# Two-layer cross attention on one core: the second layer's engine orders rewritten, with a new share-out of its copies

## The chip, the cores and the metric

The kernel runs on one core of one Trainium2 chip. The metric is device time in microseconds (us) of one execution; shorter is better. The engines of the core are named as the profile names them: PE is TensorE (matmuls and transposes), ACT is ScalarE, DVE is VectorE, POOL is GpSimd, SP is SyncE, which here only issues DMAs. Each engine runs its own instructions strictly in the order in which they are written, and waits on semaphores for the others. Two layers run one after the other with an MLP between them; the change touches only the last part, which takes the final third of the time.

## What is computed

There are 16 entries. Each has 128 rows of 512 numbers, `x`, and 128 context rows of 512. The first layer is a cross attention with MLP, which this change leaves alone. The second takes its result `x` and does, for `b, l, s = 4, 256, 256` in the reference, which for a mask of zeros and the kernel's own split of the data is 16 entries of 128 by 128:

```python
q = hidden_state @ Wq + bq              # 32 heads of 16
k = encoder_hidden_state @ Wk + bk      # 8 heads of 16, each shared by 4 query heads
v = encoder_hidden_state @ Wv + bv
scores = jnp.einsum('bkgld,bksd->bkgls', q, k) * scale
scores = scores + encoder_attention_mask[:, :, None, :, :]
attn = jax.nn.softmax(scores, axis=-1)
out = jnp.einsum('bkgls,bksd->bkgld', attn, v)
out = out.transpose(0, 3, 1, 2, 4).reshape(b, l, H)
out = out @ Wo + bo
x = out + hidden_state
mu = jnp.mean(x, axis=-1, keepdims=True)
var = jnp.var(x, axis=-1, keepdims=True)
return (x - mu) * jax.lax.rsqrt(var + EPS) * gamma + beta
```

## The kernel before

The second layer is `second_attention` (L1236). One entry is a chain of steps that goes from engine to engine. Numbers are kept in fp32, and a product of two of them is made of three passes over halves (`hi` and `lo`: a rounded copy and what the rounding left off), so nearly each matrix is written twice, `hi` by ACT and `lo` by DVE. The steps of an entry, by the functions' names:

- `turn`: PE transposes the entry's rows into bank `G[1]`; ACT writes `hThi`, DVE writes `hTlo`.
- `query`: PE, 12 matmuls of 512 columns into `G[0]`; DVE adds the bias into `Qn`. `turn_query`: PE transposes `Qn`, ACT writes `QThi`, DVE `QTlo`.
- `context`: PE, 12 matmuls of 256 columns into `G[1]` (keys and values together); DVE adds the biases (`Cn`, `V`). `turn_context`: one transpose, ACT writes `KThi`, DVE `KTlo`.
- `scores(r)`, r = 0 and 1: PE, 24 matmuls on four row strips that fill the four banks `S`. Each round feeds four steps `k`, so an entry has eight.
- `mask_max(k)` on DVE adds the mask and takes the maximum of four heads; `exp(k)` on ACT does four exponentials with their sums; `probs(k)` on PE turns the four 128x128 blocks of `pr` into bank `O` (even `k`) or `T` (odd `k`); `copy(k)` brings them into `pT`. Even copies are DVE's, odd ones ACT's.
- `invert(r)`: DVE takes the reciprocals of the sums `den`, each written 16 times over, 128x256 (L1555). `inverse(r)`: PE turns them into `G[r]`; `spread(r)`: ACT copies them into `inv` (L1455).
- `values(r)`: PE, 8 small matmuls into `G[r]`, the same bank; `attended(r)`: DVE multiplies by `inv` into `an` (L1568), and POOL makes `aThi` and `aTlo`.
- `output`: PE, two halves of 6 matmuls into `G[1]`; DVE adds the residual into `res`. `moments`, `root` (POOL, Newton steps on 128x1), `norm`, `affine` (POOL) finish the entry, and SP stores it.

The order of each engine is written out by hand in its `period(b)`. A period works on three or four entries at once: `before` is b-1, `after` b+1. The periods of b = -1, 0, 1 and 14, 15, 16 are written out; the twelve between run in a loop of two periods. The two `G` banks serve ten uses of an entry, and every use waits until the one before it in that bank has been read, by wait lines in the functions. The PE order puts `scores(after, 0)` behind both halves of `output(before)`, then `inverse(b, 0)`, `probs(b, 5)`, `values(b, 0)`, `probs(b, 6)`, `turn(b+2)`; `query` is the second step of the next period. ACT has `spread(b, 0)` behind `exp(b, 5)` and `turn_context`, and three exponentials' steps or copies behind it. DVE has `turn(b+2)`, `moments(before)` and `attended(b, 0)` near the end of its period, and the two reciprocals between masks.

Of the kernel before, what the change touches and what calls it, by code (L numbers as in the profile page):

```python
# [28 lines left out]
ALU = mybir.AluOpType  # L29
# [3 lines left out]
B, R, H = 16, 128, 512  # L33
# [1190 lines left out]

def all_periods(eng, period):

    for n in (-1, 0, 1):
        period(Entry(n))
    with eng.Fori(0, (B - 4) // 2) as it:
        period(Entry(2, it))  # L1230
        period(Entry(3, it))
    for n in (B - 2, B - 1, B):
        period(Entry(n))


def second_attention(nc, top, staging, ident, handed, banks, mask, q_b, k_b, v_b, o_b, norm_w, norm_b, out):  # L1236
# [14 lines left out]
    with st:  # L1251
# [19 lines left out]
        rec = [sb(f"rec{r}", [P, RC * EIGHT, DH1]) for r in range(ROUNDS)]  # L1271
# [15 lines left out]
        a_seen, moments_seen, scores_seen = map(sem, ("a_seen", "moments_seen", "scores_seen"))  # L1287
# [6 lines left out]
        SMALL = 3  # L1294

# [8 lines left out]
        with nc.Block() as block:  # L1304

            @block.sync
            def _(sp):
                def load_context(e):
                    for h in range(2):
# [3 lines left out]
                def load_mask(e):  # L1313
                    sp.dma_start(madd[e.s][:, :], mask[e.index(), 0]).then_inc(mask_loaded[e.s], 16)

                def load_rows(e):
                    sp.dma_start(y_rows[e.s][:, :], kept_y[e.index()]).then_inc(y_loaded[e.s], 16)
# [4 lines left out]

                def period(b):
                    if b.exists() and b.plus(2).exists():
                        sp.wait_ge(resid_ready, b.count(1, 1))
                        sp.wait_ge(turned, b.count(1, 1))
                        load_rows(b.plus(2))
                        sp.wait_ge(c_full, b.count(1, 1))
                        load_context(b.plus(2))
                    if b.plus(-2).exists():  # L1330
                        store(b.plus(-2))
                    if b.exists() and b.plus(2).exists():
                        sp.wait_ge(masked, b.count(STEPS, STEPS))
                        load_mask(b.plus(2))
# [16 lines left out]
                store(Entry(B - 1))  # L1351
# [4 lines left out]
            def _(pool):  # L1356
# [22 lines left out]

                def root(e):  # L1380
# [18 lines left out]
                def period(b):  # L1399
                    if b.plus(-2).exists():  # L1400
                        root(b.plus(-2))
                    if b.plus(-1).exists():
                        attended(b.plus(-1), 1)
                    if b.plus(-2).exists():
                        affine(b.plus(-2))
                    if b.plus(1).exists():
                        residual(b.plus(1))
                    if b.exists():
                        attended(b, 0)

                all_periods(pool, period)
                root(Entry(B - 1))
                affine(Entry(B - 1))

            @block.scalar
            def _(act):
                def turn(e):
                    act.wait_ge(turned, e.count(1, 1))
                    nc.scalar.activation(hT[0][:, :, :], G[1][:, :].rearrange("p (k r) -> p k r", k=KC), ACT.Copy)\
                        .then_inc(h_hi, 1)  # L1420

                def turn_query(e):
                    act.wait_ge(qt_full, e.count(1, 1))
                    nc.scalar.activation(QT[e.s][0][:, :, :], G[0][:, :].rearrange("p (k r) -> p k r", k=KC),
                                         ACT.Copy, scale=scale).then_inc(q_hi, 1)

                def turn_context(e):
                    act.wait_ge(ct_full, e.count(1, 1))
                    for a in range(2):
                        last = nc.scalar.activation(KT[e.s][0][:, a, :], G[0][:, 0:R], ACT.Copy,  # L1430
# [14 lines left out]
                def copy(e, k):  # L1445
                    r, j = k // SB, k % SB
                    act.wait_ge(p_full[1], e.count(SB, k // 2 + 1))
                    wait(act, o_full, e.count(ROUNDS, r - 1))
                    nc.scalar.activation(pT[r][:, j, :, :, :].rearrange("p c a k -> p (c a k)"), PT[1][:, :], ACT.Copy)\
                        .then_inc(copied[1], 1)  # L1450

                def spread(e, r):
                    act.wait_ge(r_full, e.count(ROUNDS, r + 1))
                    wait(act, a_scaled, e.count(ROUNDS, r - 1))
                    nc.scalar.activation(inv[r][:, :], G[r][:, 0:RC * R], ACT.Copy).then_inc(r_spread, 1)  # L1455

                def period(b):
                    before, after = b.plus(-1), b.plus(1)
                    if b.exists():
                        exp(b, 0)  # L1460
                    if before.exists():
                        copy(before, 7)
                    if b.exists():
                        exp(b, 1)
                    if before.exists():
                        spread(before, 1)
                    if b.exists():
                        exp(b, 2)
                        copy(b, 1)
                        exp(b, 3)  # L1470
                    if after.exists():
                        turn_query(after)
                    if b.exists():
                        exp(b, 4)
                        copy(b, 3)
                        exp(b, 5)
                    if after.exists():
                        turn_context(after)
# [3 lines left out]
                    if b.exists():  # L1482
                        spread(b, 0)
                        exp(b, 6)
                        copy(b, 5)
                    if b.plus(2).exists():
                        turn(b.plus(2))
# [545 lines left out]
```

## Time and profile before

| | us |
|---|---|
| median of three runs | 1276.95 |
| lowest and highest | 1273.9, 1278.49 |
| the profiled execution's own time | 1279.8 |
| its span in the profile | 1278.0 |
| end of the MLP, last rows added up by DVE | about 861 |
| scores of entry 1 (first matmul) | 898.22 |
| scores of entry 15 (first matmul) | 1233.17 |

The span is what the profile covers; the execution's own time is 1.8 us longer, and both are of one execution. In a timeline row the first number is the start from the span's start, the second the length; a matmul's length includes its way through the array, so back-to-back matmuls overlap, and their pace is read from start to start. `[1.33 <-DVE KT0lo L1534]` says that the engine stood idle for 1.33 us before the row and that DVE's write of `KT0lo` released it. PEclk is the clock that TensorE was granted, as a share of its upper level of 2.4 GHz; the lower level is 1.2 GHz, a share of 0.5.

### The profile page before, as it was taken

The numbers are of one execution on the slowest core, as the hardware profiler recorded it, in microseconds if no ns is written. First come the engines' busy times: TensorE is split into PE (matmuls) and PEld (weight loads), VectorE is DVE, ScalarE is ACT, GpSimd is POOL, SyncE is SP. The second block draws the span as 40 slices with busy tenths as digits, with TensorE's granted clock in tenths as the row PEclk, the third lists the DMA queues.
The fourth block names the chain that finished last, engine by engine and source line by source line (L and its number), as shares of the span: only waits on it lengthen the run. The fifth ranks groups of instructions, "written<-read, shape, count | busy, mean of one in ns | idle before, by whom it ended". The sixth has DMA issues, their size and how long they took to land. (4 is left out here: it accounts for less than half of the span.)

```text
span 1278.0 us, 27329 instructions
## 1 busy us (share of the span) xinstructions
PE 1121.2 (88%) x8976; PEld 935.1 (73%) x8976; DVE 735.7 (58%) x2667; ACT 658.9 (52%) x2220; POOL 310.3 (24%) x475
## 2 busy tenths in 40 slices
PE   4899999999999975999999999996778778778774
PEld 3788888888888854898989989985556556556553
DVE  4577777777776755422212212215678778788784
ACT  4455555555555544533333333325677677677672
POOL 1223333332332331000000000000133333333334
PEclk8999999999999987999999999997889989989987
DMA  6212111112111005211001101404111111111100
GB/s 242 86 55 69 45 43 43 43 47 81 44 43 43 26 17 174 90 50 50 30 20 49 50 0 49 116 17 116 32 59 36 53 52 35 56 49 35 45 10 25
DMA packets 65349, 71.10 MB, mean 56 GB/s; under 512 B 7056, under 2 KB 41104, under 8 KB 65296
## 3 DMA queue, kind: packets, MB, share of 16 engines
q1 hardware_dynamic: 65296, 70.42, 17.5%
q8 instruction: 30, 0.49, 0.2%
q14 instruction: 23, 0.19, 0.1%
HBM read 49.43 MB, written 20.97 MB: 55 GB/s over the span
## 5 line engine op out<-in xcount | busy, mean ns | idle before, releaser
L689 POOL TENSOR_TENSOR pr<-pr,rec 128x512 f32<-128x512 f32 x128 | 130.6, 1042 | 297.2 <-DVE rec L947 297.2
L1441 ACT ACTIVATE pr<-pr,nmax 128x128 f32<-128x128 f32 x512 | 198.1, 392 | 0.8
L1921 ACT ACTIVATE g_m<-J,b_part_m 128x256 f32<-128x256 f32 x128 | 60.6, 474 | 217.9 <-PE J L162 217.9
L791 ACT ACTIVATE pr<-pr,nmax 128x256 f32<-128x256 f32 x256 | 126.6, 501 | 4.1 <-DVE nmax L936 4.0
L1548 DVE CUSTOM_DVE_ANT_0 pr<-S,madd 128x128 f32<-128x128 f32 x512 | 115.7, 284 | 14.3 <-PE S L1700 10.3
L1898 POOL TENSOR_TENSOR resid_m<-resid_m,b_all_m 128x512 f32<-128x512 f32 x16 | 23.1, 1464 | 329.7 <-DMA resid_m<-in_x 329.7
L1441 ACT ACTIVATION_READ_ACCUMULATOR pr<-pr,nmax 128x1 f32 x512 | 98.4, 192 | 0.0
L936 DVE CUSTOM_DVE_ANT_0 pr<-S,madd 128x256 f32<-128x256 f32 x256 | 92.6, 418 | 8.2 <-PE S L1127 8.1
L162 PE MATMUL J<-wqhi,hThi 128*128 128x512 f32 x128 | 65.1, 508 | 22.6 <-DVE wqlo L150 11.3
L162 PE MATMUL J<-nT0hi_m,uphi_m 128*128 128x256 f32 x256 | 73.2, 286 | 9.8 <-DVE uplo_m L150 8.9
L162 PE MATMUL J<-hThi,wkhi 128*128 128x256 f32 x256 | 75.4, 294 | 5.9 <-DVE wvlo L150 5.9
L162 PE MATMUL J<-nT0hi_m,uplo_m 128*128 128x256 f32 x256 | 72.7, 284 | 0.0
L162 PE MATMUL J<-nT0lo_m,uphi_m 128*128 128x256 f32 x256 | 72.6, 283 | 0.0
L1710 PE MATMUL T<-ident,pr 128*128 128x128 f32 x256 | 42.0, 289 | 34.5 <-ACT pr L1441 34.5
L162 PE MATMUL J<-hThi,wklo 128*128 128x256 f32 x256 | 72.0, 281 | 0.0
L162 PE MATMUL J<-hTlo,wkhi 128*128 128x256 f32 x256 | 72.0, 281 | 0.0
L162 PE MATMUL J<-nT1hi_m,uphi_m 128*128 128x256 f32 x256 | 71.8, 280 | 0.0
L162 PE MATMUL J<-nT1hi_m,uplo_m 128*128 128x256 f32 x256 | 71.6, 280 | 0.0
L162 PE MATMUL J<-nT1lo_m,uphi_m 128*128 128x256 f32 x256 | 71.5, 279 | 0.0
L1145 PE MATMUL S<-ident,pr 128*128 128x128 f32 x512 | 62.9, 277 | 0.0
L162 PE MATMUL J<-wqlo,hThi 128*128 128x512 f32 x128 | 61.8, 483 | 0.0
L1455 ACT ACTIVATE inv<-J 128x256 f32<-128x256 f32 x32 | 12.3, 384 | 94.2 <-PE J L1720 94.2
(232 smaller groups left out, 3323.1 us busy)
## 6 DMA issues: line engine op xcount, KB each, us to landing
staged<-in_L_xattn_mlp_w SPq DMA_DIRECT2D x16, 512.0 KB, 5.1
rows<-in_ctx SPq DMA_DIRECT2D x16, 256.0 KB, 2.8
rows<-in_x SPq DMA_DIRECT2D x16, 256.0 KB, 3.0
kept_c<-hThi SPq DMA_DIRECT2D x16, 256.0 KB, 2.6
kept_c<-hTlo SPq DMA_DIRECT2D x16, 256.0 KB, 2.8
kept_n<-n_out SPq DMA_DIRECT2D x16, 256.0 KB, 2.4
n_in<-kept_n SPq DMA_DIRECT2D x16, 256.0 KB, 3.7
resid_m<-in_x SPq DMA_DIRECT2D x16, 256.0 KB, 2.9
```

The costliest lines, as they stand in the source:

```text
L162: mm = nc.tensor.matmul(out, stationary(a, k), moving(b, k), start=first and k == 0 and (a, b) == PASSES[0], stop=last and k == chunks - 1 ...
L689: pool.tensor_tensor(part, part, by.unsqueeze(2).broadcast_to([P, per_bank, keys]), ALU.mult).then_inc(normed, 1)
L791: last = nc.scalar.activation(part, part, ACT.Exp, bias=nmax[slot][:, at], scale=-1.0, accum_out=den[slot][:, at])
L936: last = nc.vector.tensor_tensor_reduce(pr[slot][:, j, cols], S[j][:, cols], madd[s][:, :], -1.0, FAR, ALU.add, ALU.min, nmax[slot][:, j * ...
L1145: mm = nc.tensor.transpose(S[j][:, to * P:(to + 1) * P], pr[slot][:, j, q * P:(q + 1) * P], ident[:, :])
L1441: last = nc.scalar.activation(pr[k][:, i, :], pr[k][:, i, :], ACT.Exp, bias=nmax[k][:, i:i + 1], scale=-1.0, accum_out=den[r][:, at:at + 1])
L1455: nc.scalar.activation(inv[r][:, :], G[r][:, 0:RC * R], ACT.Copy).then_inc(r_spread, 1)
L1548: last = nc.vector.tensor_tensor_reduce(pr[k][:, i, :], S[j][:, i * R:(i + 1) * R], madd[e.s][:, :], -1.0, FAR, ALU.add, ALU.min, nmax[k][ ...
L1710: mm = nc.tensor.transpose(PT[t][:, i * R:(i + 1) * R], pr[k][:, i, :], ident[:, :])
L1898: pool.tensor_tensor(resid[t][:, :], resid[t][:, :], b2_all[:, :], ALU.add)\
L1921: nc.scalar.activation(g[slot][:, :], J[j][:, 0:PR], ACT.Gelu_apprx_tanh, bias=b1_part[:, f, :]).then_inc(J_taken[j], 1)
```

## The change

All of it is in the second layer.

1. **Orders.** The `period` functions of all five engines are rewritten with a helper `at(b, ahead, operation, ...)` that runs an operation for entry b+ahead if there is one. `query` and `turn` are now done two entries ahead, `query(b+2)` at the very end of PE's period; `spread(b, 0)` moves behind `exp(b, 6)`; `moments` moves from b-1 to b-2 and so to the next period; `attended(b-1, 0)` opens DVE's period. The periods run from b = -2 to 17, and ten of them are in the loop.
2. **Banks.** Which of the two `G` banks a use gets is now a table (`HOME`), and the wait before a use is worked out from the order of uses (`ORDER`, `EMPTIED`) by `free`. `inverse(0)` and `values(0)`, which shared a bank, now have one each, and `output` and `values(1)` do too; `values` has lost its own wait for `spread`.
3. **Copies.** `copy(3)` moves from ACT to DVE: three of eight are ACT's (1, 5, 7), five DVE's (0, 2, 3, 4, 6).
4. **Reciprocals.** DVE takes them on 128x16; POOL then writes each 16 times over into a new tile `wide` (`widen`), which PE turns.
5. **SP.** The loads of entry b+2 carry their waits with them and stand ahead of the store of b-2.
6. **Start and end.** The turn of entry 0 stood ahead of the weights on ACT, DVE and PE. It is now in the period of b = -2, behind the weights on ACT, and on DVE behind the waits for all the constants too.

```diff
+        HOME = dict(turn=1, query=1, turn_query=1, context=0, turn_context=0, inverse0=1, inverse1=0, values0=0,
+                    values1=0, output=1)
+        ORDER = (("inverse1", -1), ("turn_query", 1), ("values1", -1), ("turn", 2), ("context", 1), ("output", -1),
+                 ("turn_context", 1), ("inverse0", 0), ("values0", 0), ("query", 2))
...
+                def widen(e, r):
+                    pool.wait_ge(rec_ready, e.count(ROUNDS, r + 1))
+                    wait(pool, r_full, e.count(ROUNDS, r - 1))
+                    pool.nop().then_inc(rec_seen, 1)
+                    pool.tensor_copy(wide[r][:, :, :], rec[r][:, :].unsqueeze(2).broadcast_to([P, RC * EIGHT, DH1]))\
+                        .then_inc(rec_wide, 1)
...
                 def invert(e, r):
                     dve.wait_ge(exped, e.count(STEPS, SB * r + SB))
-                    nc.vector.reciprocal(rec[r][:, :, :], den[r][:, :].unsqueeze(2).broadcast_to([P, RC * EIGHT, DH1]))\
-                        .then_inc(rec_ready, 1)
+                    wait(dve, rec_wide, e.count(ROUNDS, r - 1))
+                    nc.vector.reciprocal(rec[r][:, :], den[r][:, :]).then_inc(rec_ready, 1)
...
             @block.vector
...
                 def period(b):
+                    at(b, 0, mask_max, 1)
+                    at(b, -1, attended, 0)
+                    at(b, 0, mask_max, 2)
+                    at(b, -1, copy, 6)
+                    at(b, -1, invert, 1)
+                    at(b, 0, mask_max, 3)
+                    at(b, 1, query)
+                    at(b, -2, moments)
+                    at(b, 0, copy, 0)
+                    at(b, 1, turn_query)
+                    at(b, 0, mask_max, 4)
+                    at(b, -1, attended, 1)
+                    at(b, 0, mask_max, 5)
+                    at(b, 2, turn)
+                    at(b, 0, mask_max, 6)
+                    at(b, 1, context)
+                    at(b, -2, norm)
+                    at(b, 0, invert, 0)
+                    at(b, 0, mask_max, 7)
+                    at(b, 0, copy, 2)
+                    at(b, 1, turn_context)
+                    at(b, 0, copy, 3)
+                    at(b, -1, output)
+                    at(b, 0, copy, 4)
+                    at(b, 1, mask_max, 0)
...
             @block.tensor
...
                 def period(b):
+                    at(b, -1, probs, 7)
+                    at(b, -1, inverse, 1)
+                    at(b, 0, probs, 0)
+                    at(b, 1, turn_query)
+                    at(b, 0, scores, 1)
+                    at(b, 0, probs, 1)
+                    at(b, -1, values, 1)
+                    at(b, 2, turn)
+                    at(b, 0, probs, 2)
+                    at(b, 1, context)
+                    at(b, -1, output, 0)
+                    at(b, 1, turn_context)
+                    at(b, 0, probs, 3)
+                    at(b, -1, output, 1)
+                    at(b, 0, probs, 4)
+                    at(b, 1, scores, 0)
+                    at(b, 0, probs, 5)
+                    at(b, 0, inverse, 0)
+                    at(b, 0, values, 0)
+                    at(b, 0, probs, 6)
+                    at(b, 2, query)
...
             @block.scalar
...
                 def period(b):
+                    at(b, 0, exp, 1)
+                    at(b, -1, copy, 7)
+                    at(b, -1, spread, 1)
+                    at(b, 1, turn_query)
+                    at(b, 0, exp, 2)
+                    at(b, 0, copy, 1)
+                    at(b, 2, turn)
+                    at(b, 0, exp, 3)
+                    at(b, 0, exp, 4)
+                    at(b, 1, turn_context)
+                    at(b, 0, exp, 5)
+                    at(b, 0, exp, 6)
+                    at(b, 0, spread, 0)
+                    at(b, 0, exp, 7)
+                    at(b, 0, copy, 5)
+                    at(b, 1, exp, 0)
...
             @block.gpsimd
...
                 def period(b):
+                    at(b, -1, attended, 0)
+                    at(b, -1, widen, 1)
+                    at(b, -2, root)
+                    at(b, -1, attended, 1)
+                    at(b, -2, affine)
+                    at(b, 0, widen, 0)
+                    at(b, 1, residual)
```

What this does to the instructions is seen at three places of the loop. `pr5_1` is the block of step 5, `inv0_1` the spread inverses of round 0, `J0` and `J1` are the banks `G[0]` and `G[1]`, and REGISTER_ALU rows compute what a wait compares with.

ACT around the spread of round 0, before:

```order
L1430 ACTIVATE KT1hi_1<-J0,parity_1 128x128 x2
L1453 REGISTER_ALU
L1455 ACTIVATE inv0_1<-J0 128x256
L1436 REGISTER_ALU
L1441 ACTIVATE pr6_1,den1_1<-pr6_1,nmax6_1 128x128 x4
L1447 REGISTER_ALU
L1449 ACTIVATE pT1_1<-T 128x512
L1418 REGISTER_ALU
L1419 ACTIVATE hThi_1<-J1 128x512
```

ACT in the same place after the change:

```order
L1455 ACTIVATE KT1hi_1<-J0,parity_1 128x128 x2
L1461 REGISTER_ALU
L1466 ACTIVATE pr5_1,den1_1<-pr5_1,nmax5_1 128x128 x4
L1461 REGISTER_ALU
L1466 ACTIVATE pr6_1,den1_1<-pr6_1,nmax6_1 128x128 x4
L1478 REGISTER_ALU
L1480 ACTIVATE inv0_1<-J1 128x256
L1461 REGISTER_ALU
L1466 ACTIVATE pr7_1,den1_1<-pr7_1,nmax7_1 128x128 x4
```

The exponentials of steps 5 and 6 now stand ahead of `inv0`, and the turn of the next rows (`hThi`) is no longer among what follows it.

PE behind the first scores of the next entry, before:

```order
L1720 MATMUL J0<-ident,rec0_1 128x128 x2
L1707 REGISTER_ALU
L1710 MATMUL T<-ident,pr5_1 128x128 x4
L1730 MATMUL J0<-pT0_1,V0_1 32x256 x8
L1707 REGISTER_ALU
L1222 REGISTER_ALU
L1710 MATMUL O<-ident,pr6_1 128x128 x4
L1658 REGISTER_ALU
L1222 REGISTER_ALU
L1661 MATMUL J1<-ident,y_rows0 128x128 x4
L1710 MATMUL T<-ident,pr7_1 128x128 x4
```

PE in the same place after:

```order
L1717 MATMUL T<-ident,pr5_1 128x128 x4
L1659 REGISTER_ALU
L1722 REGISTER_ALU
L1724 MATMUL J1<-ident,wide0_1 128x128 x2
L1734 MATMUL J0<-pT0_1,V0_1 32x256 x8
L1714 REGISTER_ALU
L1222 REGISTER_ALU
L1717 MATMUL O<-ident,pr6_1 128x128 x4
L162 MATMUL J1<-wqhi_1,hThi_1 128x512
```

The inverses now follow the block of step 5 and go into the other bank than the values; the query product of b+2 follows the block of step 6, where the turn of the rows and the block of step 7 stood.

DVE at the reciprocal of round 1, before:

```order
L1548 ISA nmax2_1 128x1
L1560 REGISTER_ALU
L1561 COPY pT1_1<-O 128x512
L1554 ISA
L1555 RECIPROCAL rec1_1<-den1_1 128x256
```

DVE in the same place after:

```order
L1559 ISA nmax2_1 128x1
L1571 REGISTER_ALU
L1222 REGISTER_ALU
L1573 COPY pT1_1<-O 128x512
L1565 ISA
L1567 RECIPROCAL rec1_1<-den1_1 128x16
L1559 ISA pr3_1,nmax3_1<-S3,madd0_1 128x128
```

The place is the same, the reciprocal is 16 elements wide in place of 256.

## Rows read from the trace of the kernel before

**Rows 1.** The page of the kernel before, its first line.

```profile
span 1278.0 us, 27329 instructions
```

**Rows 2.** Windows: start:end us, length, busy us (instructions) by engine, PEclk, DMA share, GB/s.

```profile
core 0: us, PE busy (x) PEld busy (x) DVE busy (x) ACT busy (x) POOL busy (x), PEclk, DMA share, GB/s
560.00:850.00 290.00, 290.00 (x1859) 261.35 (x1858) 60.32 (x121) 97.62 (x212) 16.36 (x12) 1.00 0.13 40
1043.20:1138.60 95.40, 74.98 (x645) 56.47 (x643) 75.02 (x352) 66.75 (x296) 33.49 (x77) 0.93 0.14 47
1045.00:1050.20 5.20, 1.76 (x13) 1.33 (x13) 2.58 (x11) 4.43 (x21) 0.00 (x0) 1.00 0.48 151
1050.20:1054.20 4.00, 4.00 (x11) 3.14 (x12) 4.00 (x21) 2.22 (x10) 3.13 (x13) 0.59 0.00 0
1054.20:1066.00 11.80, 10.16 (x93) 7.83 (x92) 10.74 (x52) 8.49 (x38) 4.00 (x6) 1.00 0.06 22
```

**Rows 3.** Timeline, PE, first scores of entries 1, 8, 9, 15: start us, us, engine.

```profile
898.22 0.59 PE L1700 MATMUL S<-KT1hi,QT1hi 32*128 32x256 f32 x4 [3.40 <-DVE KT1lo L1534]
...
1066.06 0.39 PE L1700 MATMUL S<-KT0hi,QT0hi 32*128 32x256 f32 x4 [1.33 <-DVE KT0lo L1534]
1089.86 0.39 PE L1700 MATMUL S<-KT1hi,QT1hi 32*128 32x256 f32 x4 [1.32 <-DVE KT1lo L1534]
...
1233.17 0.39 PE L1700 MATMUL S<-KT1hi,QT1hi 32*128 32x256 f32 x4 [1.25 <-DVE KT1lo L1534]
```

**Rows 4.** Timeline of one period, ACT and DVE rows behind the scores.

```profile
1067.45 0.38 ACT L1455 ACTIVATE inv<-J 128x256 f32<-128x256 f32 x1 [3.49 <-PE J L1720]
1070.62 0.60 ACT L1419 ACTIVATE hThi<-J 128x512 fp32r<-128x512 f32 x1 [0.77 <-PE J L1661]
...
1071.25 0.69 DVE L1505 TENSOR_TENSOR hTlo<-J,hThi 128x512 fp32r<-128x512 f32 x1 [3.04 <-ACT hThi L1419]
```

**Rows 5.** The tile `rec` and its readers: count, ns min/median/max.

```profile
L947 DVE RECIPROCAL rec<-den x64: 166/169/179, 48.5 to 467.9; 128x4 f32<-128x4 f32 x64
L1555 DVE RECIPROCAL rec<-den x32: 1741/1746/1750, 894.5 to 1255.9; 128x256 f32<-128x256 f32 x32
```

**Rows 6.** Lines by form, 1043.2 to 1138.6 us, DVE, then ACT.

```profile
L1561 DVE COPY pT<-O 128x512 f32<-128x512 f32 x16 | 10.8, 673 | 1.6 <-PE O L1710 1.6
...
L1441 ACT ACTIVATE pr<-pr,nmax 128x128 f32<-128x128 f32 x128 | 49.5, 393 | 0.3
L1449 ACT ACTIVATE pT<-T 128x512 f32<-128x512 f32 x16 | 9.3, 581 | 0.0
```

**Rows 7.** Timeline, PE, one period: query product and first half of output.

```profile
1050.18 0.47 PE L162 MATMUL J<-wqhi,hThi 128*128 128x512 f32 x1 [0.72 <-DVE an L1568]
...
1054.61 0.60 PE L1710 MATMUL O<-ident,pr 128*128 128x128 f32 x4
...
1061.17 0.47 PE L1743 MATMUL J<-wohi,aT0hi 128*128 128x512 f32 x1 [0.38 <-issue]
...
1062.63 0.27 PE L1690 MATMUL J<-ident,Cn 128*128 128x128 f32 x1
```

**Rows 8.** Lines by form, same stretch, POOL.

```profile
L1376 POOL CAST aT0hi<-an 128x256 fp32r<-128x256 f32 x4 | 1.6, 397 | 20.5 <-DVE an L1568 20.5
L1378 POOL TENSOR_TENSOR aT0lo<-an,aT0hi 128x256 fp32r<-128x256 f32 x4 | 3.0, 738 | 0.3
```

**Rows 9.** Timeline, start of the layer: PE, then DVE.

```profile
866.42 0.79 PE L162 MATMUL J<-wqhi,hThi 128*128 128x512 f32 x1 [4.03 <-DVE wqlo L150]
...
872.43 0.69 DVE L1512 TENSOR_TENSOR Qn<-J,bq_all 128x512 f32<-128x512 f32 x1 [4.93 <-DMA nb_all<-in_L_xattn_beta]
879.30 2.36 DVE L150 TENSOR_TENSOR wolo<-staged,wohi 128x1024 fp32r<-128x1024 f32 x2 [0.33 <-ACT wohi L145]
```

**Rows 10.** Timeline, end: last exponential on ACT, PE, then DVE.

```profile
1255.03 0.40 ACT L1441 ACTIVATE pr<-pr,nmax 128x128 f32<-128x128 f32 x1
...
1258.94 1.93 PE L1730 MATMUL J<-pT,V 128*32 128x256 f32 x16 [0.47 <-ACT inv L1455]
...
1266.56 0.69 DVE L1575 TENSOR_TENSOR res<-J,resid 128x512 f32<-128x512 f32 x1 [4.74 <-PE J L1743]
```

More of the change, by code:

```diff
@@ L1222, in wait, with at @@
         eng.wait_ge(sem, value)
+def at(b, ahead, operation, *which):
+    e = b.plus(ahead)
+    if e.exists():
+        operation(e, *which)
 def all_periods(eng, period):
-    for n in (-1, 0, 1):
+    for n in range(-2, 4):
         period(Entry(n))
[L1229 to L1232, printed above, removed]
+    with eng.Fori(0, (B - 6) // 2) as it:
+        period(Entry(4, it))
+        period(Entry(5, it))
+    for n in range(B - 2, B + 2):
         period(Entry(n))
@@ L1308, in load_context @@
                 def load_context(e):
+                    wait(sp, c_full, e.count(1, -1))
                     for h in range(2):
@@ L1321, in store, with first_two @@
                     sp.dma_start(out[e.index()], fin[e.s][:, :]).then_inc(stored[e.s], 16)
+                def first_two(e):
+                    return e.it is None and e.n < 2
                 def period(b):
[L1324 to L1334, printed above, removed]
+                    if not first_two(b.plus(2)):
+                        at(b, 2, load_context)
+                    if not first_two(b.plus(2)):
+                        at(b, 2, load_rows)
+                    if not first_two(b.plus(2)):
+                        at(b, 2, load_mask)
+                    at(b, -2, store)
                 for s in range(2):
@@ L1454, in spread @@
                     wait(act, a_scaled, e.count(ROUNDS, r - 1))
-                    nc.scalar.activation(inv[r][:, :], G[r][:, 0:RC * R], ACT.Copy).then_inc(r_spread, 1)
+                    nc.scalar.activation(inv[r][:, :], bank(f"inverse{r}")[:, 0:RC * R], ACT.Copy).then_inc(r_spread, 1)
                 def period(b):
[L1458 to L1478, printed above, removed]
+                    at(b, 0, exp, 1)
[14 more added lines that the diff above has]
+                    at(b, 1, exp, 0)
                     if b.it is None and b.n == -1:
@@ L1481, in period @@
                             staging.take_hi(nc, act, u, targets[u])
[L1482 to L1487, printed above, removed]
-                    if b.exists():
-                        exp(b, 7)
-                turn(Entry(0))
                 for u in QUERY + (CONTEXT,):
@@ L1652, in _, with free @@
                 all_periods(dve, period)
-                norm(Entry(B - 1))
             @block.tensor
             def _(pe):
+                def free(use, e):
+                    at_ = [name for name, _ in ORDER].index(use)
+                    b = e.plus(-ORDER[at_][1])
+                    for back in range(1, 3 * len(ORDER)):
+                        periods, n = divmod(at_ - back, len(ORDER))
+                        name, ahead = ORDER[n]
+                        user = b.plus(periods + ahead)
+                        if HOME[name] == HOME[use] and user.exists():
+                            sem_, per, more = EMPTIED[name]
+                            pe.wait_ge(sem_, user.count(per, more))
+                            return
                 def turn(e):
                     pe.wait_ge(y_loaded[e.s], e.uses(16))
-                    wait(pe, res_ready, e.count(1, -2))
+                    free("turn", e)
                     for k in range(KC):
-                        mm = nc.tensor.transpose(G[1][:, k * R:(k + 1) * R], y_rows[e.s][:, k * P:(k + 1) * P],
+                        mm = nc.tensor.transpose(bank("turn")[:, k * R:(k + 1) * R], y_rows[e.s][:, k * P:(k + 1) * P],
                                                  ident[:, :])
@@ L1724, in values @@
                 def values(e, r):
[L1725 removed]
+                    free(f"values{r}", e)
                     for t in range(2):
@@ L1775, in period @@
-                    if b.exists():
-                        probs(b, 4)
-                    if before.exists():
-                        output(before, 1)
-                    if after.exists():
-                        scores(after, 0)
-                    if b.exists():
-                        inverse(b, 0)
-                        probs(b, 5)
-                        values(b, 0)
-                        probs(b, 6)
-                    if b.plus(2).exists():
-                        turn(b.plus(2))
```

164 lines of the change are left out of this document (45 added, 119 removed).

## The prediction

> **What bounds the kernel now.** The span [rows 1] is read first, and of it only the last third can change. There the starts of the first scores give the beat: 898.22 us for entry 1, 1233.17 for entry 15 [rows 3], 14 periods of 23.9 us. Next comes the busy time in a stretch of four such periods, 95.40 us [rows 2]: PE 74.98, DVE 75.02, ACT 66.75, POOL 33.49, which is 18.7, 18.8, 16.7 and 8.4 us for one period of 23.85. No engine is full, so the period is a ring of waits. The timeline shows the ring. PE waits 1.33 us for `KTlo` at 1066.06. Behind those scores stand the inverses, and ACT has idled 3.49 us for them when it spreads them at 1067.45. ACT then does one step of exponentials and a copy, waits 0.77 us for the turned rows, writes `hThi` at 1070.62, and DVE, idle for 3.04 us, takes it at 1071.25 [rows 4]. From there DVE works nearly without a gap up to the next `KTlo` and the scores at 1089.86 [rows 3]. DVE's reciprocals lie in that last part.
>
> There is a second price. At the end of the idle part PE has been busy for 1.76 us of 5.20; its clock then stands at a share of 0.59 for 4 us, most of it the lower level, and the query product falls there [rows 2]. That product of 12 matmuls takes 4.43 us (1050.18 to 1054.61). Six matmuls of the same width take 1.46 us in the output (1061.17 to 1062.63), so twelve would take about 2.9 at the upper level [rows 7]. The wait thus costs 1.5 us more on PE in each period.
>
> **The change, part by part.** I first ask how short a period can be by each engine's own work, then whether the waits allow it.
>
> DVE. Two reciprocals of 1.746 us shrink to 128x16. The first layer's 128x4 form takes 0.169 us; the 252 elements between the two forms cost 1.577 us, so 12 more than four give 0.24 us [rows 5]. That takes off 3.0 us. One more copy adds 0.67 us as shown, some 0.60 from start to start [rows 6]. 18.8 - 3.0 + 0.6 = 16.4 us.
>
> ACT. One copy less, 0.58 us shown [rows 6], 0.5 in the queue: 16.7 - 0.5 = 16.2 us.
>
> PE. No matmul is added or dropped. If it no longer idles long, the query product is back at 2.9: 18.7 - 1.5 = 17.2 us. That counts the tails of matmuls before each idle piece; adding up starts in the dense part of a period gives some 16.5. So PE's floor is 16.5 to 17.2.
>
> POOL. Two widenings of 128x256 are new, in a form that the trace of before does not have. The nearest rows are a cast of 128x256 at 0.40 us and a subtraction with two inputs at 0.74 [rows 8]; I take 0.4, with 0.4 and 0.8 as ends, since the copy too has one input. POOL ends near 9.2 to 10 us, far below the others, and its cover matters only for who waits: `widen(1)` lies between DVE's reciprocal and PE's `inverse(1)`, and `widen(0)` behind `affine`.
>
> Do the waits allow some 17 us? I lay the two new orders of DVE and PE side by side, with the step lengths above and 0.2 us for a hand-over, and ask by how much PE's period must start later than DVE's. What DVE hands to PE asks for the following offsets: the reciprocal with its widening 3.6 us, `Qn` 3.7, `QTlo` 3.8, `an` of round 1 before the context product 4.0, `hTlo` before the output 4.0, `KTlo` before the scores 3.9. What PE hands to DVE allows at most: `values(1)` before `an` 4.3, the turned rows by way of ACT 4.3, the context product 4.4, the scores before the next `mask_max(0)` 4.3, the output before `res` 4.5. So an offset of 4.0 to 4.3 meets all of them. ACT needs 3.5 to 3.85 against DVE and may have at most 3.6, so it will stand a little at the spread, and it has 0.8 us of room for that in a period of 17. The step that held the ring before, the spread of round 0, now has `exp(6)` ahead of it, so its wait of 3.49 us is covered by an exponential step of about 1.5 us (four at 0.39 from start to start [rows 6]) and by the earlier inverses; what comes late next is PE's own queue. The windows are only 0.3 us wide, so I add a little and take 17.0 us a period, with 16.4 and 17.9 as its ends.
>
> The moved loads on SP cost nothing: rows and context of b+2 are asked for about a period before they are used. The store of b-2 now stands behind them; nobody waits for it except POOL two entries on.
>
> The start. The turn of entry 0 now waits for the last constant. DVE took that at 872.43 for `Qn` [rows 9]; it will now take it for `hTlo`, 0.7 us, then the query product follows, 4.4 us at the lower level as in [rows 7], where it had begun at 866.42 [rows 9]. `Qn` comes near 878, 5.5 us later. The turn of entry 1 now precedes the scores of entry 0, and the split of the output weights, 2.36 us on DVE at 879.30 [rows 9], now follows `mask_max(0)` and so holds up `mask_max(1)`. Against this, the query of entry 1 is already done. I take the scores of entry 1 at 904.5, 6.3 us later; ends 3 and 9.
>
> The end. In before, the last exponential starts at 1255.03 [rows 10], 21.9 us behind the scores of entry 15. In the new order ACT has its eight exponential steps (12.3 us), four smaller things (1.5) and short waits: it ends some 18.5 us behind those scores, 3.8 less with the reading-out of the sum. Of what follows up to 1278.0, 22.6 us, `invert` and `widen` take 0.7 instead of 1.75, so the values at 1258.94 [rows 10] come 1.1 us earlier; `output`, which ends with `res` at 1266.56 [rows 10], the moments, the root and the store stay. Scores of entry 15 to the end: 18.5 + 21.5 = 40 us, where it was 44.8.
>
> **The sum.** 904.5 + 14 x 17.0 + 40 = 1182.5 us of span, 95.5 less than before. With 1.8 us outside the span this is 1184.3 against the profiled execution's own 1279.8. That execution was 2.85 us above the median, so I forecast 1182 us (0.926 of before). The period's ends alone move it by -8 and +13 us, start and end by -4 and +4: 1172 to 1196.
>
> **Rivals.** *The clock falls once in each period.* For it: after the query product PE now has the blocks of steps 7, 0, 1 and 2, two small products, turned inverses, `Qn` and rows in one run of about 5 us before the next wide product, and the same kind of work left the clock at 0.59 behind 1045 to 1050.2. Against it: there PE stood idle for most of the time, and the dense stretch 1054.20 to 1066.00, with 10.16 of 11.80 us busy and a good third of that in transposes, was granted 1.00 [rows 2]. If it falls, the query product's 1.5 us come back, on context and output instead: 18.6 us a period, 1205 us. The Trainium skill speaks for this rival, in TensorE: Matmul & The Clock Gate, Part 4: PE-mode transpose: transposes do not count as activity for the clock as other matmuls do. The stretch at 1.00 does not bear it out, and the stretch before the fall cannot tell it from idleness.
>
> *The waits still make a ring and only the reciprocals' gain stays.* For it: three engines within 5% of each other, and windows of 0.3 us. Both reciprocals lie in the old ring, 3.0 us of it, and 23.9 - 3.0 = 20.9 would be left. 904.5 + 14 x 20.9 + 40 gives 1237 us as the worst of this case; anything between 18.5 and 21 us a period belongs to it or to the clock. Against it: the spread, which held the ring, has been passed by an exponential step, and the queue positions leave the slack counted above.
>
> *Slower.* PE stays at the lower level for most of every period, since many short waits of 0.1 to 0.3 us lie between its steps. At that level matmuls take twice as long from start to start, 16.5 us of work becomes up to 30 and the time 904.5 + 14 x 30 + 40 = 1364 us. It passes the old 23.9 when a bit more than half of PE's work falls at the lower level. Against it: the MLP, with PE always busy, had 1.00 for 290 us, and in the old period a gap of several us cost the clock for only 4 us of 24 [rows 2].
>
> *No gain.* The orders wait for something that I have overlooked, such as a load of SP or POOL's `root` ahead of `attended(1)`, and the period stays near 23.9; with the longer start it would be about 1278.
>
> **How the numbers follow.** Forecast (1172 to 1196): 0.60. Clock: 0.17. Ring: 0.15. Slower: 0.04. No gain: 0.03, and 0.01 is left for below 1172. The range reaches from 1169 up to 1215, which takes in the clock rival and the nearer part of the ring, 0.85 or so. A measurement can tell about 0.3% (4 us) from no change; faster by more than that 0.94, within it 0.02, slower 0.04.
>
> **What would show it.** Scores of one entry 17.0 us behind those of the last, PE busy for over 93% of the period at a share of 1.00, ACT's wait before `inv` below 0.6 us where it was 3.49, and DVE's before `hTlo` below 0.3 us. A query or output product that takes over 4 us is the clock rival. A DVE that is under 85% busy together with a PE under 90% is the ring, and the wait that is longest names it. `widen` above 0.8 us, or first scores of entry 1 outside 901 to 908, would make single terms wrong. The forecast as a whole is wrong if the period is above 17.9 us or below 16.4.

## The result, and the profile after

| | before | after |
|---|---|---|
| median, us | 1277.65 | 1174.83 |
| lowest and highest | 1273.9, 1278.49 | 1172.35, 1180.94 |
| runs | 4 | 4 |
| scores of entry 1, profiled execution | 898.22 | 906.43 |
| scores of entry 15 | 1233.17 | 1136.74 |
| one period between them, mean of 14 | 23.93 | 16.45 |
| from scores of entry 15 to the end | 44.8 | 38.0 |

The ratio is 0.921, with an interval of 0.917 to 0.925. The forecast was 1182 us. The profiled execution took 1176.46 us. Its span stands beside [rows 1]:

```profile
span 1174.7 us, 27388 instructions
## 1 busy us (share of the span) xinstructions
PE 1085.1 (92%) x8976; PEld 918.0 (78%) x8976; DVE 691.9 (59%) x2683; ACT 648.2 (55%) x2204; POOL 321.9 (27%) x507
```

The windows, with the columns of [rows 2]: twelve periods, then a short stretch that is rich in transposes, then all that follows the scores of entry 15.

```profile
939.34:1136.80 197.46, 197.25 (x1933) 156.05 (x1932) 190.99 (x1069) 191.58 (x877) 110.35 (x254) 1.00 0.20 64
1043.80:1046.62 2.82, 2.82 (x41) 2.38 (x40) 2.29 (x12) 2.82 (x13) 0.04 (x2) 1.00 0.00 0
1136.74:1174.70 37.96, 21.58 (x189) 13.64 (x188) 20.58 (x102) 19.09 (x89) 21.95 (x56) 0.86 0.08 29
```

In twelve periods PE stands still for 0.21 us, at a granted clock of 1.00 throughout. A period of 16.46 us holds 16.44 of PE, 15.9 of DVE, 16.0 of ACT and 9.2 of POOL. The ring of waits (each engine held up by another, round to the first) is gone, and the second layer runs at the pace of PE's own work. PE's timeline in the middle of it, where before every score stood behind a wait [rows 3] and the query product began behind one [rows 7]:

```profile
1038.07 0.39 PE L1707 MATMUL S<-KT1hi,QT1hi 32*128 32x256 f32 x4
...
1039.47 0.38 PE L1724 MATMUL J<-ident,wide 128*128 128x128 f32 x2
1039.78 1.07 PE L1734 MATMUL J<-pT,V 128*32 128x256 f32 x16
...
1041.20 0.48 PE L162 MATMUL J<-wqhi,hThi 128*128 128x512 f32 x1
...
1044.08 0.60 PE L1717 MATMUL T<-ident,pr 128*128 128x128 f32 x4
1044.52 0.38 PE L1724 MATMUL J<-ident,wide 128*128 128x128 f32 x2
1044.74 0.60 PE L1717 MATMUL O<-ident,pr 128*128 128x128 f32 x4
1045.17 0.60 PE L1682 MATMUL J<-ident,Qn 128*128 128x128 f32 x4
```

No row carries a bracket, so nothing waited. The query product takes 2.88 us from its start to the next step's, where it took 4.43. A block of four transposes takes 0.43 to 0.44 us; with eight blocks, the turns of the rows and of `Qn` (four each), two pairs of inverses at 0.22 and one more transpose, transposes are over a quarter of a period. The waits of the old ring, ACT's two and DVE's one of [rows 4], read so now, with DVE's longest behind them:

```profile
1032.44 0.60 ACT L1444 ACTIVATE hThi<-J 128x512 fp32r<-128x512 f32 x1 [0.28 <-PE J L1666]
...
1039.89 0.38 ACT L1480 ACTIVATE inv<-J 128x256 f32<-128x256 f32 x1 [0.18 <-PE J L1724]
...
1044.28 0.69 DVE L1523 TENSOR_TENSOR Qn<-J,bq_all 128x512 f32<-128x512 f32 x1 [0.26 <-PE J L162]
```

3.49 us before `inv` have become 0.18, and DVE does not wait for `hThi` at all. The reciprocal and the copy that took over its width, as in [rows 5] (count, ns min/median/max):

```profile
L1567 DVE RECIPROCAL rec<-den x32: 240/243/247, 904.1 to 1154.8; 128x16 f32<-128x16 f32 x32
L1407 POOL COPY wide<-rec x32: 387/397/406, 904.5 to 1155.4; 128x256 f32<-128x256 f32 x32
```

The start of the layer, DVE and then PE, which answers to [rows 9]:

```profile
872.10 0.69 DVE L1516 TENSOR_TENSOR hTlo<-J,hThi 128x512 fp32r<-128x512 f32 x1 [6.20 <-DMA nb_all<-in_L_xattn_beta]
878.04 0.69 DVE L1523 TENSOR_TENSOR Qn<-J,bq_all 128x512 f32<-128x512 f32 x1 [5.25 <-PE J L162]
...
891.80 2.36 DVE L150 TENSOR_TENSOR wolo<-staged,wohi 128x1024 fp32r<-128x1024 f32 x2 [2.66 <-ACT wohi L145]
...
897.44 0.69 PE L1682 MATMUL J<-ident,Qn 128*128 128x128 f32 x4 [4.60 <-DVE Qn L1523]
...
906.43 0.39 PE L1707 MATMUL S<-KT1hi,QT1hi 32*128 32x256 f32 x4
```

The first turn waits for the last constant, as the prediction had it. The split of the output weights costs more than it had: ACT's `wohi` is late by 2.66 us, DVE stands behind it with `wolo` until 894.2, and three steps of masks and `Qn` of entry 1 stand behind that, so PE idles 4.60 us. The end, ACT, PE, DVE, against [rows 10]:

```profile
1154.27 0.40 ACT L1466 ACTIVATE pr<-pr,nmax 128x128 f32<-128x128 f32 x1
...
1156.98 1.70 PE L1734 MATMUL J<-pT,V 128*32 128x256 f32 x16 [0.64 <-ACT inv L1480]
...
1163.27 0.69 DVE L1587 TENSOR_TENSOR res<-J,resid 128x512 f32<-128x512 f32 x1 [2.81 <-PE J L1746]
```

From the scores of entry 15 to the values it was 25.8 us and is 20.2; from there to the end 19.1 and is 17.7.

So the balance of the two spans is: the 14 periods 334.95 - 230.31 = 104.6 us less, start 8.2 more, end 6.9 less, together 103.3.

### The profile page after: what moved, and what is told of

Its sections match the earlier page's. It is cut to its first block and busy times, and to the rows that moved or that the text cites. A ratio compares the mean times of both kernels' runs of the same rounds, so it can differ in the third digit from the quotient of the medians.

```text
span 1174.7 us, 27388 instructions
## 1 busy us (share of the span) xinstructions
PE 1085.1 (92%) x8976; PEld 918.0 (78%) x8976; DVE 691.9 (59%) x2683; ACT 648.2 (55%) x2204; POOL 321.9 (27%) x507
## 5 line engine op out<-in xcount | busy, mean ns | idle before, releaser
L162 PE MATMUL J<-wqhi,hThi 128*128 128x512 f32 x128 | 56.6, 442 | 18.9 <-DVE hTlo L1516 11.0
L1145 PEld LDWEIGHTS S<-ident,pr 128*128 128x128 f32 x512 | 58.6, 143 | 2.3 <-issue 0.2
L162 PEld LDWEIGHTS J<-nT0hi_m,uphi_m 128*128 128x128 f32 x256 | 49.1, 192 | 13.0 <-issue 9.4
L162 PEld LDWEIGHTS J<-hThi,wkhi 128*128 128x128 f32 x256 | 49.1, 192 | 7.9 <-DVE wvlo L150 5.1
```

Of the source, the lines that this page charges most:

```text
L162: mm = nc.tensor.matmul(out, stationary(a, k), moving(b, k), start=first and k == 0 and (a, b) == PASSES[0], stop=last and k == chunks - 1 ...
L1145: mm = nc.tensor.transpose(S[j][:, to * P:(to + 1) * P], pr[slot][:, j, q * P:(q + 1) * P], ident[:, :])
```

## The experiments

The ratio stands after each median, with its interval, against runs of the kernel before on the same chip. Periods are means of the 14 from entry 1 to entry 15 in the profiled execution. The MLP's end moves by up to 10 us from one execution to the next in kernels whose code is the same up to there, so starts are counted from DVE's write of the MLP's last rows (`y_out`): the scores of entry 1 come 38.7 us behind it in before (859.53 to 898.22) and 47.3 in after (859.10 to 906.43).

### The two halves of the change, each alone

`e1_wide_recip` is after with DVE's wide reciprocals back:

```diff
...
-                    wait(dve, rec_wide, e.count(ROUNDS, r - 1))
-                    nc.vector.reciprocal(rec[r][:, :], den[r][:, :]).then_inc(rec_ready, 1)
+                    wait(dve, r_full, e.count(ROUNDS, r - 1))
+                    nc.vector.reciprocal(rec[r][:, :, :], den[r][:, :].unsqueeze(2).broadcast_to([P, RC * EIGHT, DH1]))\
+                        .then_inc(rec_ready, 1)
...
```

> The new orders with the reciprocals as they were: DVE takes them on 128x256, and POOL does not widen. Theory (the new order makes the period as long as the busiest engine's work, PE's 16.45 us): DVE goes from 16.0 to 19.0 us of work in a period and becomes the bound, so the period is 19.0 to 19.5 us and the time 1174.8 + 14 x 2.8 = 1214 us, more if PE's waits bring its clock down. Rival (the order did it alone, reciprocals lie in DVE's slack): under 17 us a period, below 1183 us.

1221.0 us, 0.956 [0.953, 0.959], period 19.11. The window from 939 to 1104 us, columns of [rows 2]:

```profile
939.00:1104.00 165.00, 147.81 (x1398) 111.44 (x1396) 162.84 (x774) 138.77 (x632) 74.36 (x168) 1.00 0.18 60
```

DVE is busy 99% of the time: 15.9 + 3.0 of reciprocals = 18.9 us of its work in a period of 19.1. It is the bound, and PE, 10% idle in pieces of up to 1.3 us, keeps its clock at 1.00. The period is the one worked out; the time is 7 us above the 1214 us expected, since the sum left start and end as in after, and they are longer by 1.5 us (entry 1's scores 48.8 us behind `y_out`) and 3.3 us (41.3 us behind the scores of entry 15, where after has 38.0).

`e2_small_recip_old_order` is before with the small reciprocals and `widen` on POOL, and nothing else:

```diff
...
-                    nc.vector.reciprocal(rec[r][:, :, :], den[r][:, :].unsqueeze(2).broadcast_to([P, RC * EIGHT, DH1]))\
-                        .then_inc(rec_ready, 1)
+                    wait(dve, rec_wide, e.count(ROUNDS, r - 1))
+                    nc.vector.reciprocal(rec[r][:, :], den[r][:, :]).then_inc(rec_ready, 1)
...
```

> The kernel before with the reciprocals alone changed: 128x16 on DVE, widened by POOL. Theory (the old period is a ring of waits through DVE's queue, in which both reciprocals lie): 3.0 us off each of 15 periods, 20.9 us a period, 1277 - 45 = 1232 us, and the query product still falls at the lower clock behind PE's wait. Rival (the ring closes through another engine as soon as DVE is shorter): 22 to 23.5 us a period, 1250 to 1272 us.

1266.2 us, 0.991 [0.988, 0.994], period 23.55 in a profiled execution that was itself 9 us above the median. The theory (1232) missed; the rival was right. Of 3.0 us taken from DVE in each period at most 0.9 came back (13.1 us between the medians, over 14 periods). Windows of seven periods, of the query product and of the idle part ahead of it; the timeline there (PE, DVE, ACT); and a line of the table of waits over the seven periods (us in total, times, longest):

```profile
939.00:1104.00 165.00, 134.54 (x1134) 101.34 (x1133) 112.52 (x622) 117.30 (x522) 64.08 (x148) 0.90 0.15 48
1141.90:1146.60 4.70, 4.55 (x14) 3.56 (x15) 3.23 (x26) 2.44 (x11) 2.72 (x10) 0.64 0.00 0
1137.00:1142.00 5.00, 1.75 (x12) 1.27 (x12) 2.52 (x9) 4.23 (x19) 0.00 (x0) 1.00 0.46 157
```

```profile
1142.05 0.47 PE L162 MATMUL J<-wqhi,hThi 128*128 128x512 f32 x1 [0.66 <-DVE an L1581]
1147.10 0.69 DVE L1574 COPY pT<-O 128x512 f32<-128x512 f32 x1 [1.97 <-PE O L1723]
1147.32 0.38 ACT L1468 ACTIVATE inv<-J 128x256 f32<-128x256 f32 x1 [2.90 <-PE J L1733]
```

```profile
ACT inv L1468 <- PE J L1733: 42.0, 14, 3.5
```

By these rows the ring closes again by another way. PE's query product waits for `an` to empty its bank, runs 4.4 us because the clock has fallen to 0.64, and the block of step 0, which DVE's copy wants, and the turned inverses, which ACT wants, stand behind it on PE. DVE got faster and waits: it is busy for 68% of the time, where in before it is 79% [rows 2]. ACT's waits for the inverses are nearly what they were (42.0 us, 44.6 in before). No run took the query product out of this way, so that it is the one that sets the period is read from the timeline and not tried.

So neither half alone gives the gain. The orders alone give 58 us, the reciprocals alone 13, and both 103. The reciprocals are worth 46 us in the new orders, where DVE's queue sets the period without them.

`e9_spread_alone` is before with only the spread of round 0 behind the exponentials of step 6:

```diff
-                        spread(b, 0)
                         exp(b, 6)
+                        spread(b, 0)
```

> The kernel before with one move alone: ACT's spread of round 0 behind exp(6). Theory (the old ring closes through several steps, so one move gives only what the next one leaves): probs(6) no longer waits 0.54 us and the rows are turned that much earlier, 0.6 us a period, 1277 - 9 = 1268 us. Rival (the spread held the ring alone): its wait of 3.49 us shrinks to about 1.9 and the period with it, 22.3 us, 1253 us.

1268.2 us, 0.994 [0.991, 0.996], as expected; the period, 23.08 in the profiled execution, is 0.85 us shorter where 0.6 was worked out. ACT's waits for the inverses in seven periods are only a quarter shorter than in before, whose line over the same stretch comes first:

```profile
ACT inv L1455 <- PE J L1720: 44.6, 14, 3.5
...
ACT inv L1455 <- PE J L1720: 32.4, 14, 2.9
```

### Single steps of the new order, moved back

`e4_spread_early` puts the spread ahead of step 6 in after:

```diff
-                    at(b, 0, exp, 6)
                     at(b, 0, spread, 0)
+                    at(b, 0, exp, 6)
```

> The changed kernel with one step of ACT moved back: the spread of round 0 ahead of exp(6), as in the kernel before. Theory: ACT then waits 1.8 us for the inverses (they are ready at 1039.89, it gets there at 1038.06), and the ring inverse, spread, six exponential steps or so, hThi, hTlo, output, inverse closes at 17.3 us a period: 1174.8 + 15 x 0.8 = 1187 us. Rival (ACT has room, the place of the spread is nothing): 1175 us.

1193.2 us, 0.935 [0.932, 0.939], period 17.56. ACT's wait is back, and the block of step 6 is late on PE:

```profile
1046.73 0.39 ACT L1480 ACTIVATE inv<-J 128x256 f32<-128x256 f32 x1 [1.69 <-PE J L1724]
...
1048.77 0.65 PE L1717 MATMUL O<-ident,pr 128*128 128x128 f32 x4 [1.08 <-ACT pr L1466]
```

`e5_one_bank` gives values(0) the bank of the inverses again:

```diff
-        HOME = dict(turn=1, query=1, turn_query=1, context=0, turn_context=0, inverse0=1, inverse1=0, values0=0,
+        HOME = dict(turn=1, query=1, turn_query=1, context=0, turn_context=0, inverse0=1, inverse1=0, values0=1,
...
```

> The changed kernel with values(0) in the bank of inverse(0), as the kernel before had it; the waits follow from the table. Theory: PE waits 0.5 us for ACT's spread before the values and a little for DVE's an before the query product, 17.0 to 17.2 us a period, 1174.8 + 15 x 0.65 = 1185 us, clock at 1.00. Rival (banks are nothing): 1175 us.

1188.3 us, 0.930 [0.927, 0.932], period 17.37. The direct wait is small (table of waits, 939 to 1104 us); PE is idle for 6.1 of these 165 us in all:

```profile
PE J L1734 <- ACT inv L1480: 4.7, 10, 0.5
```

`e10_attended_early` puts attended(0) at the end of DVE's own period, behind copy(4), in place of behind mask_max(1) of the next:

```diff
-                    at(b, -1, attended, 0)
...
                     at(b, 0, copy, 4)
+                    at(b, 0, attended, 0)
                     at(b, 1, mask_max, 0)
```

> The changed kernel with one step of DVE moved back: attended(b, 0) at the end of period b, as in the kernel before, in place of behind mask_max(1) of the next. Theory: DVE then waits 1.3 us for values(0) in every period (they are ready at 1040.85, its queue is there at 1039.54) and has only 0.45 us of room, so 17.3 us a period, 1187 us. Rival (DVE has room enough): 1175 us.

1195.0 us, 0.936 [0.933, 0.938], period 17.59. DVE waits for the values, and by way of the later reciprocal and `widen` PE waits too:

```profile
1049.16 0.42 DVE L1580 TENSOR_TENSOR an<-J,inv 128x256 f32<-128x256 f32 x1 [1.30 <-PE J L1734]
...
1053.57 0.44 PE L1724 MATMUL J<-ident,wide 128*128 128x128 f32 x2 [0.65 <-POOL wide L1407]
```

Each of the three costs 0.9 to 1.15 us a period, 13 to 20 us in time. In e4 and e10 that is 0.3 us a period more than was worked out, in e5 0.2 more than its upper end.

### The share of copies, and less work for PE

`e3_copy3_act` gives copy(3) back to ACT:

```diff
                     at(b, 1, turn_context)
+                    at(b, 0, copy, 3)
                     at(b, 0, exp, 5)
...
-                    at(b, 0, copy, 3)
                     at(b, -1, output)
```

> The changed kernel with copy(3) back on ACT, behind turn_context: four copies each. Theory (PE is the bound, ACT and DVE have 0.46 us of room): ACT goes from 16.0 to 16.4 us and just fits; 16.45 to 16.7 us a period, 1175 to 1179 us. Rival (the share of copies is what made the orders fit): ACT's waits for PE stay on top of its work, 16.9 us or more a period, 1181 us or more.

1177.1 us, 0.919 [0.917, 0.921], beside 1176.1 for after itself (below), period 16.47:

```profile
939.00:1104.00 165.00, 165.00 (x1615) 130.70 (x1614) 155.22 (x883) 164.19 (x744) 91.58 (x211) 1.00 0.20 68
```

ACT is now as full as PE and the period has not moved. The new share of copies earns nothing as long as PE is the bound.

`e6_less_pe` leaves out the third pass of the output product, four matmuls an entry:

```diff
-                        for a, b in PASSES:
+                        for a, b in PASSES[:2]:
...
```

> The changed kernel with less work for PE: the output product leaves out its third pass (the low half of the attended values), 8 matmuls of 512 columns in place of 12, so 0.93 us less PE work in a period. Theory (PE's work sets the period now, and DVE and ACT stand just behind it at 16.0 us): the period falls from 16.45 only to 16.0 to 16.2, 1169 to 1171 us. Rival (something else than PE's work sets it): no change, 1175 us. Rival (DVE and ACT have more room than their busy time says): 15.5 us a period, 1162 us.

1169.8 us, 0.916 [0.914, 0.919], period 16.29:

```profile
939.00:1104.00 165.00, 161.03 (x1581) 122.84 (x1580) 160.58 (x901) 161.47 (x740) 92.08 (x212) 1.00 0.21 69
```

Four matmuls at 0.23 us from start to start, 0.9 us, were taken from PE and 0.16 us of period came back, a little less than the theory's 0.25 to 0.45. All three engines are then 97 to 98% busy, and short waits for each other hold them (PE's longest is 0.3 us). The gain is read from the trace: the interval of the ratio overlaps that of after (0.916 to 0.921, below), so the times do not show it.

### The start

`e7_start` turns entry 0 ahead of the weights on ACT and DVE, as before:

```diff
-                    at(b, 2, turn)
+                    if b.it is not None or b.n != -2:
+                        at(b, 2, turn)
...
+                turn(Entry(0))
```

> The changed kernel with the turn of entry 0 ahead of the weights on ACT and DVE again. Theory: the query product of entry 0 starts near 866 instead of 872.9, Qn near 872 instead of 878, and the whole layer moves 5.5 us ahead: 1169 us. Rival (the start is hidden behind the output weights, whose split waits for exp(0)): 1173 to 1175 us.

`e8_start_out` is e7 with the output weights split earlier: ACT's half behind its turn of entry 1, and DVE's in two parts, behind its turn of entry 1 and behind `turn_context` of entry 0.

```diff
                     at(b, 2, turn)
+                    if b.it is None and b.n == -1:
+                        staging.take_lo(nc, dve, OUT[0], targets[OUT[0]])
...
                     at(b, 1, turn_context)
+                    if b.it is None and b.n == -1:
+                        staging.take_lo(nc, dve, OUT[1], targets[OUT[1]])
...
                     at(b, 1, mask_max, 0)
-                    if b.it is None and b.n == -1:
-                        for u in OUT:
-                            staging.take_lo(nc, dve, u, targets[u])
```

> As e7_start, and the output weights are split in the gaps of ACT and DVE before the first scores instead of behind exp(0) and mask_max(0). Theory: another 2 to 3 us, 1166 us. Rival: the split now stands ahead of KThi and KTlo, which delays the first scores by as much as is won later: same as e7_start.

After was run beside them:

> The changed kernel once more, so that the three beside it can be compared on the same chip: 1175 us.

After gave 1176.1 us, 0.919 [0.916, 0.921]; e7 1170.2, 0.914 [0.912, 0.917]; e8 1166.9, 0.912 [0.909, 0.914]. From `y_out` to the scores of entry 1 it is 47.5 us in after, 42.5 in e7 and 38.1 in e8. PE rows of e7, then of e8, from the turned query of entry 1 on; each read from its own span, whose `y_out` is at 857.50 and 853.44:

```profile
890.49 1.09 PE L1686 MATMUL J<-ident,Qn 128*128 128x128 f32 x4 [4.12 <-DVE Qn L1525]
...
899.98 0.39 PE L1711 MATMUL S<-KT1hi,QT1hi 32*128 32x256 f32 x4
```

```profile
883.51 0.63 PE L1687 MATMUL J<-ident,Qn 128*128 128x128 f32 x4 [0.44 <-DVE Qn L1525]
...
891.55 0.39 PE L1712 MATMUL S<-KT1hi,QT1hi 32*128 32x256 f32 x4
```

e7 still has the wait behind the split weights, 4.12 us; in e8 it is 0.44. So the first turn's place costs 5.0 us and the output weights' place 4.4, and with both put right the new order starts as early as the old one (38.7). e8 beats both kernels. In its profiled execution 1.5 us are lost again behind the scores of entry 15 (39.5 us where after has 38.0); the cause stays open.

## Why the prediction was right, step by step

**The period.** The main step held. The forecast had 17.0 us, with 16.4 and 17.9 as ends; 16.45 was measured, just above the lower end. PE's own work, "some 16.5" by the sum of starts, is the period, and PE is idle for 0.02 us of it. DVE's 16.4 and ACT's 16.2 came out at 15.9 and 16.0: the busy times of before hold tails that vanish when rows stand back to back. For DVE this can be read: the lengths of its rows, added up, fell by 2.3 us a period (24.6 to 22.4), near the 2.4 worked out, while its busy time fell by 2.8. The mis-sized term is the allowance for windows, 0.5 us a period added to the floor: it measured 0, and made the sum 14 x 0.55 = 7.7 us too long. That the windows are narrow is borne out in part: e4, e5 and e10 each leave one of them and pay 0.9 to 1.15 us a period at once. These steps make waits of 1.7, 0.5 and 1.3 us, so a width of 0.3 us was not measured. Narrow windows that were met cost nothing here.

**The single prices.** The reciprocal was worked out at 0.24 and took 0.243; `widen` 0.4 and took 0.397; the query product 2.9 and took 2.88. POOL's 9.2 was given as 9.2 to 10.

**The start.** The sum had 904.5 us, 6.3 later than before; it was 906.43, 8.2 later. The first half (`Qn` near 878) is exact. The term too small is the output weights': the sum counted DVE's 2.36 us but not that ACT's half ahead of it is late by 2.66. Beyond the 5.5 us of the first turn it left 0.8 for the rest; e7 and e8 measure 5.0 for the turn and 4.4 for the output weights. The whole is inside the ends of 3 and 9 us.

**The end.** 40 us were worked out and 38.0 came. ACT's last exponential step is over some 18.0 us behind the scores (18.5 expected). The rest took 19.9 us in place of 21.5, mainly since the values to `res` took 6.3 us where they took 7.6 before, which the sum had left as it was. Start and end miss by 2 us each in opposite directions and by luck cancel, so the whole miss of the profiled execution, 1176.5 against 1184.3, is the period's. The ends of the terms, added up straight, are 1170 and 1199 us, a little wider than the 1172 to 1196 given.

**The clock rival** (18.6 us a period) did not come. The stretch behind the query product, two blocks, turned inverses, turned `Qn` and the second scores, was granted 1.00 (1043.80 to 1046.62, above), and so were all twelve periods. The whole run that the rival named, from the query product's end to the next context product, is the first window here; 3.2 of its 5.1 us are transposes, from start to start. The two behind it are from the end of after:

```profile
1044.08:1049.17 5.09, 5.09 (x68) 3.96 (x66) 4.61 (x21) 4.82 (x21) 1.85 (x10) 1.00 0.00 0
1153.53:1157.00 3.47, 1.62 (x17) 1.05 (x13) 2.53 (x9) 2.59 (x10) 1.71 (x5) 1.00 0.01 2
1158.00:1160.00 2.00, 2.00 (x11) 1.16 (x4) 0.52 (x2) 0.00 (x0) 1.34 (x7) 0.50 0.03 8
```

By the Trainium skill, TensorE: Matmul & The Clock Gate, Part 4: PE-mode transpose, transposes do not count as activity for the clock as other matmuls do; no stretch of this kernel shows it with PE kept busy, though transposes are over a quarter of each period. In the periods the clock was below 1.00 only behind idleness: 0.59 behind PE busy 1.76 of 5.20 us [rows 2], 0.64 behind 1.75 of 5.00 in e2. e1 with PE 10% idle and e4 with 6%, in pieces, kept 1.00. In the end of after it fell to the lower level behind a stretch with PE busy 1.62 of 3.47 us, idle in two pieces of 1.21 and 0.64 us, and nearly all of that work was transposes. So idleness and the mix of work were not tried apart: wherever the clock fell in the periods, the little that PE did was mostly transposes too.

**The ring rival** was the weakest piece of reasoning. Its price, 23.9 less the 3.0 us of the reciprocals, is wrong: e2 shows that the old order with them keeps 23.0 to 23.6 us. A ring is as long as its slowest way round, and a second way, by e2's timeline over the query product's bank and PE's queue, was nearly as long as the first. In the same manner e9 shows that passing the spread by one step, which the prediction named first, frees little by itself. The forecast was right on this since it laid out all engines' queues side by side and did not subtract savings from the old period. That no ring is left is seen in after itself, in PE's 0.02 us of idleness a period.

**The slower rival and no gain.** No short wait of PE is left that could lower the clock, and the loads of SP, which now stand ahead of the store, hold nobody up in twelve periods. The price of the lower level was a little too high: matmuls of 512 columns follow each other by 0.43 us there and by 0.23 at the upper level (first query product and those of the loop), 1.8 times and not twice.

**The signs.** PE busy over 93% at 1.00: 99.9%. ACT's wait before `inv` below 0.6: at most 0.3. DVE's before `hTlo` below 0.3: none. The scores of entry 1 between 901 and 908: 906.4. A period of 17.0: 16.45, inside its bounds.

## What to carry to other kernels

When no engine is full, forecast a new order from the fullest engine's own work, counted from start to start, and test with each hand-over whether the queues allow it; do not subtract what was shortened from the old period, since the next ring may be nearly as long (3.0 us off DVE gave 0.9 at most in the old order, and 2.7 in the new). Once all the windows were met, no allowance for them was needed here, while each one missed cost about 1 us of 16. A reordering for the loop also moves the start: what stood ahead of the weights and constants should be left there (here 5 us), and weights that are needed later should not be split in front of work that is waited for (here 4 us).

## What the runs showed of the hardware

TensorE kept 1.00 through 197 us in which over a quarter of its time was transposes, and in e1 also with a tenth of its time idle in pieces of up to 1.3 us; in the end of after it fell to the lower level behind 3.47 us with PE busy for 1.62, nearly all of it transposes. A DVE reciprocal of 128x4 took 167 ns, of 128x16 243 and of 128x256 1746, so beyond a fixed part it went by width, some 6 ns an element (243 - 167 over 12, 1746 - 243 over 240). A GpSimd copy that writes 16 numbers 16 times over, 128x256, took 397 ns, no more than its plain cast of the same width [rows 8], while VectorE was busy for 97% of the time.
